# The power of the norms in three parts, and the next image's jobs in other slots

## The chip, the cores and the metric

One core of a Trainium2 chip runs the whole program. The metric is the device time of one execution in microseconds. The kernel before took 2167.36 us (median of three runs, 2160.34 to 2170.95).

## The reference

The program is a small vision tower on 16 images of 3 x 256 x 256, in float32:

```
h = template_match(x)              # 31x31 normalised correlation, mean over 3 channels -> 16 x 256 x 256
t = h * rsqrt(mean(h*h) + eps) * norm_w
q = (t @ Wq)  -> 16 heads of 64;  k, v = (t @ Wkv) -> 8 heads of 64 each
q, k = l2norm(q) * scale_q, l2norm(k) * scale_k       # one norm per token and head
a = softmax(causal(tanh(q k^T / 50) * 50 / 8))        # two query heads share a key head
h = layernorm(h + (a v) @ Wout)
h = layernorm(h + mlp(h))          # three hidden layers of 1024, silu gate, two gelus
```

Each image has 256 tokens of 256 values. For every token the l2norm needs 24 sums of squares (16 query heads, 8 key heads) and their power -1/2.

## The kernel before

There are three stages, one behind the other: the template correlation (`token_stage`), the attention (`attention_stage`) and the three-layer network (`mlp_stage`). The change lies in the attention alone.

Images are taken in four groups of four (`GI` = 4). For an image, the attention has 16 `make` jobs on TensorE: `make 0` to `2` project the first 128 tokens to queries and keys and `make 3` to values, `make 4` to `7` do the same for the other 128 tokens. Each is six matmuls of 512 columns (line 1041). Between them the norms are taken, once per block of 128 tokens, numbered `tb` 0 and 1: ScalarE squares `raw` (line 880); VectorE reduces the squares to 24 sums per token (`sum`, line 933); GpSimd clips them and raises them to -1/2 (`root`, lines 812 and 814); VectorE multiplies queries and keys with them (`scale`, lines 940 and 942, the keys twice). Then `make 8` to `15` transpose the scaled queries and keys (line 1053): 8, 9, 10, 11 need `scale 0`, and 12 to 15 need `scale 1`.

The attention of an image goes head by head, eight of them. For the head numbered n over the group, `score` n is eight matmuls into one of two pairs of `sim` banks (line 1065); ScalarE applies tanh and exp (lines 891 and 894); GpSimd multiplies the diagonal blocks with a triangular mask (line 820); and `mix` (line 1079) multiplies with the values. The mix of head n-2 stands behind the score of head n. All mixes write one PSUM bank, `mixed`. VectorE reads it out with a reciprocal (line 957) and a product (line 959), and the next mix on TensorE waits for that product by `s_mixread`; a sum (line 962) follows.

The engines run one list of steps, `attention_order`, each engine taking from it what is its own, strictly in this order. The list is written out by hand: at head h of an image, behind its score and mix, come the steps of `SLOTS[h]` for the next image. At the first head of an image the mix comes ahead of the score. For the last image of a group the slots lie one head later, and the last slot lies behind the second of the two mixes that follow the last score. The next group's `rms` norm has its sum at the 18th head of a group, its power on GpSimd (lines 804 and 806) two heads later, and its scaling on VectorE (line 921) four heads later. The very first image is made ahead of all heads, by `first_order`. In the list of the final group there is no image to make beside its last image.

Every job writes one of three PSUM banks and waits until the job three before was read out. Queries are read out by ScalarE and keys by VectorE (line 950). DMAs are issued by SyncE alone here, for tokens, results and a scan of words that VectorE folds in with `bits` (line 968).

Of the kernel before, what the change touches and what calls it, by code (L numbers as in the profile page):

```python
# [9 lines left out]
ALU = mybir.AluOpType  # L10
# [21 lines left out]
D, QH, HEADS, DH = SIDE, 16, 8, 64  # L32
# [52 lines left out]
def settle(eng, sem):  # L85

    eng.sem_inc(sem, 1)


def token_stage(nc, sh, X, XT, TF, TPAD, H, WORDS, WEIGHTS, WQKV, NW, GQ, GK):  # L90
# [489 lines left out]


NH = GI * HEADS
SLOTS = (
    [("make", 0), ("make", 1), ("make", 2)],
    [("sum", 0), ("root", 0), ("make", 4)],
    [("make", 5), ("make", 6), ("scale", 0)],
    [("sum", 1), ("root", 1), ("make", 3), ("make", 8)],
    [("make", 9), ("make", 10)],
    [("make", 11), ("make", 7), ("scale", 1)],
    [("make", 12)],  # L590
    [("make", 13), ("make", 14), ("make", 15)],
)


def first_order():

    order = [("turn_h", k) for k in range(4)]
    order += [("make", 0, j) for j in (0, 1, 2)] + [("sum", 0, 0), ("root", 0, 0)]
    order += [("make", 0, j) for j in (4, 5, 6)] + [("scale", 0, 0), ("sum", 0, 1), ("root", 0, 1)]
    order += [("make", 0, j) for j in (3, 7, 8, 9, 10, 11)] + [("scale", 0, 1)]  # L600
    return order + [("make", 0, j) for j in (12, 13, 14, 15)]

# [76 lines left out]
def attention_stage(nc, sh, H, WO, WORDS, X1, fine):  # L679
# [7 lines left out]
    QK = KV + HEADS * DH  # L687
    with ExitStack() as ctx:
# [13 lines left out]
        rn = sb("rn", [P, 2, QK // DH])  # L702
# [19 lines left out]
        s_settle = sh.s_settle  # L722
# [65 lines left out]
        @block.gpsimd  # L788
        def _(pool):
            pool.memset(v[:], 1.0).then_inc(s_const, 1)  # L790
            pool.memset(mask[:], 1.0).then_inc(s_const, 1)
            pool.wait_ge(s_const, 2)
            pool.affine_select(out=mask[:], in_=mask[:], compare_op=ALU.is_ge, fill=0.0, base=0,
                               pattern=[[1, P]], channel_multiplier=-1).then_inc(s_const, 1)
            pool.wait_ge(s_const, 3)

            def emit(run, g):
                for step in run.order:
                    kind = step[0]
                    if kind == "rms_root":  # L800
                        n = g + run.ahead
                        pool.wait_ge(s_hsum, n + 1)
                        settle(pool, s_settle)
                        pool.tensor_scalar(rms[:], ss[:], 1.0 / D, EPS_RMS, ALU.mult, ALU.add).then_inc(s_hmean, 1)
                        pool.wait_ge(s_hmean, n + 1)
                        pool.tensor_tensor(rms[:], rms[:], neg_half[:, 0:PR], ALU.pow).then_inc(s_hroot, 1)
                    elif kind == "root":
                        tb = step[2]
                        t = image(g, step[1]) * 2 + tb
                        pool.wait_ge(s_ss, t + 2)  # L810
                        settle(pool, s_settle)
                        pool.tensor_scalar(rn[:, tb], rn[:, tb], 1e-24, None, ALU.max).then_inc(s_clip, 1)
                        pool.wait_ge(s_clip, t + 1)
                        pool.tensor_tensor(rn[:, tb], rn[:, tb], neg_half[:], ALU.pow).then_inc(s_rn, 1)
                    elif kind == "score":
                        n = step[1]
                        pool.wait_ge(s_exp, g * NH + n + 1)
                        diag = probs[:, n % 4].rearrange("p m (b i) -> p m b i", b=3)[:, :, 0:3:2]
                        both = mask[:].rearrange("p (m b i) -> p m b i", m=1, b=1).to_broadcast([P, 2, 2, P])
                        pool.tensor_tensor(diag, diag, both, ALU.mult).then_inc(s_mask, 1)  # L820
                if run.before:
                    pool.wait_ge(s_aggr, g + 1)
                    settle(pool, s_settle)
                    pool.tensor_scalar(rstd[:], moments[:, :, 1], EPS_LN, None, ALU.add).then_inc(s_lneps, 1)
                    pool.wait_ge(s_lneps, g + 1)
                    pool.tensor_tensor(rstd[:], rstd[:], neg_half[:, 0:PR], ALU.pow).then_inc(s_rstd, 1)

            every_part(pool, emit)
            pool.wait_ge(s_lows, 2)
            pool.partition_all_reduce(lows[:, 1:2], lows[:, 0:1], P, bass.bass_isa.ReduceOp.max).then_inc(s_lows, 1)  # L830
# [76 lines left out]
        def _(dve):  # L907
# [7 lines left out]
            def emit(run, g):  # L915
                for step in run.order:
# [13 lines left out]
                    elif kind == "sum":  # L930
                        tb = step[2]
                        dve.wait_ge(s_sq, image(g, step[1]) * 2 + tb + 1)
                        dve.reduce_sum(rn[:, tb], squares[:, 0:QK].rearrange("p (h d) -> p h d", d=DH), AX_X)\
                           .then_inc(s_ss, 1)
                    elif kind == "scale":
                        tb = step[2]
                        dve.wait_ge(s_rn, image(g, step[1]) * 2 + tb + 1)
                        heads = raw[:, tb].rearrange("p (h d) -> p h d", d=DH)
                        by = rn[:, tb].rearrange("p (h d) -> p h d", d=1)
                        dve.tensor_tensor(heads[:, 0:QH], heads[:, 0:QH], by[:, 0:QH].to_broadcast([P, QH, DH]), ALU.mult)  # L940
                        for m in range(2):
                            ins = dve.tensor_tensor(keys[:, tb, :, m], heads[:, QH:],
                                                    by[:, QH:].to_broadcast([P, HEADS, DH]), ALU.mult)
                        ins.then_inc(s_qn, 1)
                    elif kind == "make" and step[2] >= 8 and step[2] % 4 >= 2:
                        img, tb, r = step[1], step[2] // 4 - 2, step[2] % 4 - 2
                        bank = read_out(run, g, step).rearrange("p (h t) -> p h t", t=P)
                        dve.wait_ge(s_score, image(g, img) * HEADS + 8)
                        by = gamma[:, 4 * r:4 * r + 4].rearrange("p (h t) -> p h t", t=1).to_broadcast([P, 4, P])
                        dve.tensor_tensor(kt[:, img % 2, 4 * r:4 * r + 4, P * tb:P * tb + P], bank, by,  # L950
                                          ALU.mult).then_inc(s_emptied["keys"], 1)
                    elif kind == "mix":
                        n = step[1]
                        img, hd = n // HEADS, n % HEADS
                        got = mixed[:, 0:4 * (DH + 1)].rearrange("p (b m d) -> p b m d", b=2, m=2)
                        dve.wait_ge(s_mix, g * NH + n + 17)
                        dve.reciprocal(rl[:], got[:, :, :, DH:DH + 1]).then_inc(s_rl, 1)
                        dve.wait_ge(s_rl, g * NH + n + 1)
                        dve.tensor_tensor(parts[:], got[:, :, :, 0:DH], rl[:].to_broadcast([P, 2, 2, DH]),
                                          ALU.mult).then_inc(s_mixread, 1)  # L960
                        dve.wait_ge(s_mixread, g * NH + n + 2)
                        dve.tensor_tensor(o[:, img % 2, :, hd], parts[:, :, 0], parts[:, :, 1],
                                          ALU.add).then_inc(s_o, 1)
                    elif kind == "bits":
                        c = g * CHUNKS + step[1]
                        dve.wait_ge(s_words, c * 16 + 16)
                        dve.wait_ge(s_bits, c + 1)
                        dve.tensor_tensor(bits[:], bits[:], words[:], ALU.bitwise_or).then_inc(s_bits, 1)
                    elif kind == "project":
                        k = step[1]  # L970
                        if k == 0:
                            dve.wait_ge(s_h, g * 16 + 16)
                        bank = read_out(run, g, step).rearrange("p (a c) -> p a c", a=2)
                        dve.tensor_tensor(h[:, 2 * k:2 * k + 2], bank, h[:, 2 * k:2 * k + 2], ALU.add)\
                           .then_inc(s_emptied["dve"], 1)
                        dve.wait_ge(s_emptied["dve"], run.emptied_before(g, "dve") + run.counts[run.jobs[step]][1])
                        for a in range(2 * k, 2 * k + 2):
                            ins = dve.bn_stats(stats[:, a], h[:, a])
                        if k == 3:
                            ins.then_inc(s_stats, 1)  # L980
# [542 lines left out]
```

## Time and profile before

| | |
|---|---|
| median of the runs | 2167.36 us |
| profiled execution: time, span | 2172.09, 2170.3 us |
| mean granted TensorE clock over the span | 0.918 |
| TensorE busy | 1915.2 us (88%) |
| VectorE busy | 1214.9 us (56%) |
| ScalarE busy | 854.4 us (39%) |
| GpSimd busy | 773.6 us (36%) |

The page gives for each engine how long it was busy. Of more use here are the views by stage, the waits, and the timelines of each engine. A timeline row has the start in us from the span's start, the duration in us of one instruction or of a run of like ones, engine, line, operation, what was written and read, the count, and in brackets the idle time of the engine just before it, with what ended it. The clock is given as a share of full speed: 1.00 is 2.4 GHz, 0.50 is 1.2 GHz.

### The profile page before, as it was taken

The page shows a single profiled execution, that of the slowest core. Times are in us where ns is not written, and L with a number is a line of the kernel's source. Part 1 is how long each engine was busy: PE and PEld are TensorE (multiplying, and loading weights), DVE is VectorE, ACT ScalarE, POOL GpSimd, SP SyncE. Part 2 cuts the span into 40 slices and gives each one's busy share as a digit, 9 for nine tenths or more (in the row PEclk, how much of TensorE's full clock was granted, in tenths as well). Part 3 has the DMA queues.
Part 4 walks back from the last instruction along what each step waited for, and adds up shares of the span by engine and source line. Part 5 has one row for each costly group of instructions (what it writes and reads, how often), then busy time and mean ns, then how long its engine had stood idle before and what let it go on. Part 6 is the DMA issues. An engine that isn't in the chain of part 4 may idle for free. (4 is left out here: it accounts for less than half of the span.)

```text
span 2170.3 us, 31220 instructions
## 1 busy us (share of the span) xinstructions
PE 1915.2 (88%) x11768; PEld 1651.7 (76%) x11768; DVE 1214.9 (56%) x1671; ACT 854.4 (39%) x1164; POOL 773.6 (36%) x515
## 2 busy tenths in 40 slices
PE   4788998988948988998899899859999999999997
PEld 4788888888946777777778677748787877877876
DVE  7999999899944564565565554532413314134141
ACT  5553443445234563665355545512222212222121
POOL 3223222122254443554254344414333333243332
PEclk9899999999977898897998898879999999999999
DMA  9122212112101000200100010023000000000000
GB/s 143 71 93 77 108 45 91 71 45 117 59 29 53 21 15 8 79 21 14 67 21 21 8 59 14 21 112 144 20 1 19 19 0 19 0 19 20 1 10 11
DMA packets 32211, 95.87 MB, mean 44 GB/s; under 512 B 18630, under 2 KB 18758, under 8 KB 26569
## 3 DMA queue, kind: packets, MB, share of 16 engines
q1 hardware_dynamic: 31500, 89.80, 13.0%
q10 hardware_dynamic: 576, 4.19, 0.5%
q8 instruction: 93, 1.52, 0.3%
q14 instruction: 42, 0.34, 0.0%
HBM read 81.37 MB, written 24.15 MB: 49 GB/s over the span
## 5 line engine op out<-in xcount | busy, mean ns | idle before, releaser
L554 PE MATMUL conv<-w_hi,x_hi 128*128 128x368 f16 (+5 forms) x1320 | 358.0, 280 | 8.5 <-POOL w_lo L262 4.8
L554 PE MATMUL conv<-w_lo,x_hi 128*128 128x368 f16 (+5 forms) x1320 | 358.5, 280 | 0.0
L554 PE MATMUL conv<-w_hi,x_lo 128*128 128x368 f16 (+5 forms) x1320 | 356.8, 280 | 0.0
L820 POOL TENSOR_TENSOR probs<-probs,mask 128x512 f32<-128x512 f32 x128 | 177.6, 1392 | 299.1 <-ACT probs L894 299.1
L1079 PE MATMUL mixed<-v,probs 128*128 128x65 f32 x1536 | 231.2, 308 | 24.2 <-POOL probs L820 15.0
L1079 PEld LDWEIGHTS mixed<-v,probs 128*128 128x128 f32 x1536 | 214.7, 221 | 41.4 <-POOL probs L820 16.8
L1253 POOL TENSOR_TENSOR ha_lo<-raw_c,ha_hi 128x512 fp32r<-128x512 f32 x128 | 165.0, 1289 | 209.9 <-DVE ha_hi L1303 209.9
L1291 ACT ACTIVATE raw_c<-ring,sh 128x512 f32<-128x512 f32 x128 | 88.1, 688 | 372.7 <-PE ring L1388 372.6
L1388 PE MATMUL ring<-ha_hi,wh 128*128 128x512 f32 x512 | 209.4, 409 | 16.8 <-POOL ha_lo L1253 16.8
L554 PEld LDWEIGHTS conv<-w_hi,x_hi 128*128 128x128 f16 x1320 | 192.9, 146 | 17.6 <-issue 9.5
L1388 PE MATMUL ring<-ha_lo,wh 128*128 128x512 f32 x512 | 206.2, 403 | 0.0
L1388 PE MATMUL ring<-hb_hi,wh 128*128 128x512 f32 x512 | 202.5, 396 | 0.0
L1388 PE MATMUL ring<-hb_lo,wh 128*128 128x512 f32 x512 | 201.7, 394 | 0.0
L1303 DVE CAST ha_hi<-raw_c 128x512 fp32r<-128x512 f32 x128 | 80.7, 631 | 213.3 <-ACT raw_c L1291 211.1
L554 PEld LDWEIGHTS conv<-w_hi,x_lo 128*128 128x128 f16 x1320 | 193.4, 147 | 8.4 <-issue 0.3
L554 PEld LDWEIGHTS conv<-w_lo,x_hi 128*128 128x128 f16 x1320 | 193.1, 146 | 8.7 <-issue 0.2
L451 DVE RECIPROCAL rinv<-std 128x2048 f32<-128x2048 f32 x12 | 155.4, 12953 | 0.4
L413 DVE TENSOR_TENSOR_SCAN box<-lines 128x271 f32<-128x271 f32 x192 | 146.1, 834 | 6.7 <-ACT lines L330 6.7
L1303 DVE CAST hb_hi<-raw_c 128x512 fp32r<-128x512 f32 x64 | 27.4, 428 | 216.0 <-ACT raw_c L1291 216.0
L280 POOL TENSOR_TENSOR total<-total,part 128x512 f32<-128x512 f32 x32 | 46.9, 1477 | 262.3 <-DVE part L467 262.3
L891 ACT ACTIVATE probs<-sim 128x768 f32<-128x768 f32 x128 | 103.7, 810 | 93.2 <-PE sim L1065 92.4
L1253 POOL TENSOR_TENSOR hb_lo<-raw_c,hb_hi 128x512 fp32r<-128x512 f32 x64 | 82.5, 1289 | 161.1 <-DVE hb_hi L1303 161.1
(144 smaller groups left out, 3929.2 us busy)
## 6 DMA issues: line engine op xcount, KB each, us to landing
xt<-x_columns_in SPq DMA_DIRECT2D x12, 1163.0 KB, 5.2
xp<-x_patches_in SPq DMA_DIRECT2D x12, 1152.0 KB, 5.1
hidden_words<-hidden_weights_in SPq DMA_DIRECT2D x8, 1408.0 KB, 9.2
words<-hidden_words SPq DMA_DIRECT2D x32, 352.0 KB, 3.1
wh<-hidden_words SPq DMA_DIRECT2D x2, 4096.0 KB, 21.3
tokens<-result ACTq DMA_DIRECT2D x4, 1024.0 KB, 5.3
lines<-tokens SPq DMA_DIRECT2D x4, 1024.0 KB, 5.6
h<-tokens SPq DMA_DIRECT2D x4, 1024.0 KB, 7.7
```

Source lines behind the costliest of these rows:

```text
L280: ins = pool.tensor_tensor(total[:, :, cols], total[:, :, cols], part[:, :, cols], ALU.add)
L413: return dve.tensor_tensor_scan(out, line[:, TH:TH + SCAN], line[:, 0:SCAN], 0.0, ALU.add, ALU.subtract)
L451: dve.reciprocal(rinv[:], std[:]).then_inc(s_point, 1)
L554: ins = pe.matmul(out, xs[:, c, RI - 1 - i:RI - 1 - i + NR, :, x].rearrange("p r g -> p (r g)"), w, start=(t == 0), stop=(t == len(terms) ...
L820: pool.tensor_tensor(diag, diag, both, ALU.mult).then_inc(s_mask, 1)
L891: act.activation(probs[:, n % 4], sim[:, n % 2, :, 0:3 * P], ACT.Tanh, scale=1.0 / CLAMP).then_inc(s_tanh, 1)
L1079: ins = pe.matmul(out, probs[:, n % 4, m, at:at + P], v[:, img % 2, jb, hd], start=(jb == 0), stop=(jb == ib), skip_group_check=True)
L1253: pool.tensor_tensor(dst[1][:, u % KH], raw[:, u % 4], dst[0][:, u % KH].bitcast(F32), ALU.subtract).then_inc(s_lo, 1)
L1291: act.activation(raw[:, u % 4], bank, ACT.Gelu, scale=scale[:, m:m + 1]).then_inc(s_gelu, 1)
L1303: dve.tensor_copy(dst[0][:, u % KH], raw[:, u % 4]).then_inc(s_hi, 1)
L1388: ins = pe.matmul(bank, a, b, start=start, stop=False, skip_group_check=True)
```

## The change

`root` is no longer one step per block of 128 tokens but three (`ROOTS = 3`), each the power of 8 of the 24 columns. The first of the three also does the wait for the sums and the clip. `scale` waits until all three parts of its block are done. The slots are written anew:

```diff
+ROOTS = 3
 SLOTS = (
     [("make", 0), ("make", 1), ("make", 2)],
-    [("sum", 0), ("root", 0), ("make", 4)],
-    [("make", 5), ("make", 6), ("scale", 0)],
-    [("sum", 1), ("root", 1), ("make", 3), ("make", 8)],
-    [("make", 9), ("make", 10)],
-    [("make", 11), ("make", 7), ("scale", 1)],
-    [("make", 12)],
-    [("make", 13), ("make", 14), ("make", 15)],
+    [("sum", 0), ("make", 4), ("root", 0)],
+    [("make", 5), ("make", 6), ("root", 1)],
+    [("root", 2), ("scale", 0), ("sum", 1), ("make", 3)],
+    [("root", 3), ("root", 4), ("make", 7)],
+    [("root", 5), ("make", 8), ("make", 9)],
+    [("scale", 1), ("make", 10), ("make", 11)],
+    [("make", 12), ("make", 13), ("make", 14), ("make", 15)],
 )
```

```diff
 # first_order
-    order += [("make", 0, j) for j in (0, 1, 2)] + [("sum", 0, 0), ("root", 0, 0)]
-    order += [("make", 0, j) for j in (4, 5, 6)] + [("scale", 0, 0), ("sum", 0, 1), ("root", 0, 1)]
+    order += [("make", 0, j) for j in (0, 1, 2)] + [("sum", 0, 0)] + [("root", 0, k) for k in range(ROOTS)]
+    order += [("make", 0, j) for j in (4, 5, 6)] + [("scale", 0, 0), ("sum", 0, 1)] + [("root", 0, ROOTS + k) for k in range(ROOTS)]
```

```diff
 # GpSimd
                     elif kind == "root":
-                        tb = step[2]
+                        tb, part = step[2] // ROOTS, step[2] % ROOTS
                         t = image(g, step[1]) * 2 + tb
-                        pool.wait_ge(s_ss, t + 2)
-                        settle(pool, s_settle)
-                        pool.tensor_scalar(rn[:, tb], rn[:, tb], 1e-24, None, ALU.max).then_inc(s_clip, 1)
-                        pool.wait_ge(s_clip, t + 1)
-                        pool.tensor_tensor(rn[:, tb], rn[:, tb], neg_half[:], ALU.pow).then_inc(s_rn, 1)
+                        size = QK // DH // ROOTS
+                        cols = slice(part * size, part * size + size)
+                        if part == 0:
+                            pool.wait_ge(s_ss, t + 2)
+                            settle(pool, s_settle)
+                            pool.tensor_scalar(rn[:, tb], rn[:, tb], 1e-24, None, ALU.max).then_inc(s_clip, 1)
+                            pool.wait_ge(s_clip, t + 1)
+                        pool.tensor_tensor(rn[:, tb, cols], rn[:, tb, cols], neg_half[:, cols], ALU.pow).then_inc(s_rn, 1)
 # VectorE
-                        dve.wait_ge(s_rn, image(g, step[1]) * 2 + tb + 1)
+                        dve.wait_ge(s_rn, image(g, step[1]) * (2 * ROOTS) + (tb + 1) * ROOTS)
```

The order of the steps on each engine follows from the list: `root 0` to `2` are the parts of the first block, behind the mask products of heads 1, 2 and 3; `root 3` and `4` stand behind that of head 4, and `root 5` behind that of head 5. On VectorE `scale 0` and `sum 1` stand together behind the mix reading of slot 3.

## Rows read from the trace of the kernel before

**Rows 1.** Stages: stretch, its length, busy us of PE, PEld, DVE, ACT, POOL; PEclk; DMA

```profile
670.00:1430.00 760.00, 679.90 (x4137) 578.27 (x4136) 421.67 (x719) 406.20 (x559) 327.68 (x200) 0.87 0.09 28
...
939.65:949.50 9.85, 9.85 (x48) 9.09 (x48) 3.84 (x9) 2.85 (x4) 1.27 (x1) 0.53 0.13 38
```

**Rows 2.** Waits, 670 to 1430: who waited for whom, us in total, times, longest

```profile
PE job L1053 <- DVE keys L942: 39.6, 18, 3.2
...
PE mixed L1079 <- POOL probs L820: 15.0, 8, 3.8
PE mixed L1079 <- DVE parts L959: 9.1, 9, 1.9
```

**Rows 3.** Timeline of TensorE, 921 to 949, the second image of a group

```profile
921.93 0.92 PE L1065 MATMUL sim<-qt,kt 64*128 64x256 f32 x8
...
925.62 0.60 PE L1053 MATMUL job<-ident,raw 128*128 128x128 f32 x4
926.15 0.92 PE L1065 MATMUL sim<-qt,kt 64*128 64x256 f32 x8
...
935.23 1.55 PE L1079 MATMUL mixed<-v,probs 128*128 128x65 f32 x12 [0.76 <-POOL probs L820]
939.65 1.12 PE L1053 MATMUL job<-ident,raw 128*128 128x128 f32 x4 [2.87 <-DVE keys L942]
...
942.28 2.82 PE L1079 MATMUL mixed<-v,probs 128*128 128x65 f32 x12
...
947.45 2.15 PE L1079 MATMUL mixed<-v,probs 128*128 128x65 f32 x12
```

**Rows 4.** Timeline of ScalarE: the exponential of head 3 of the same image

```profile
924.96 0.85 ACT L894 ACTIVATE probs<-probs 128x768 f32<-128x768 f32 x1
```

**Rows 5.** Timeline of GpSimd beside the same image

```profile
917.75 4.19 POOL L814 TENSOR_TENSOR rn<-rn,neg_half 128x24 f32<-128x24 f32 x1
921.91 1.26 POOL L820 TENSOR_TENSOR probs<-probs,mask 128x512 f32<-128x512 f32 x1
...
933.91 5.13 POOL L820 TENSOR_TENSOR probs<-probs,mask 128x512 f32<-128x512 f32 x3
```

**Rows 6.** Timeline of VectorE, 897 to 940

```profile
897.45 1.21 DVE L940 TENSOR_TENSOR raw<-raw,rn 128x1024 f32<-128x1024 f32 x1
...
919.22 0.18 DVE L957 RECIPROCAL rl<-mixed 128x4 f32<-128x4 f32 x1 [2.02 <-PE mixed L1079]
...
919.90 0.29 DVE L962 TENSOR_TENSOR o<-parts 128x128 f32<-128x128 f32 x1
...
921.97 2.29 DVE L940 TENSOR_TENSOR raw<-raw,rn 128x1024 f32<-128x1024 f32 x1 [1.78 <-POOL rn L814]
924.18 1.28 DVE L942 TENSOR_TENSOR keys<-raw,rn 128x512 f32<-128x512 f32 x2
...
927.46 1.74 DVE L933 TENSOR_REDUCE rn<-lines 128x24 f32<-128x1536 f32 x1
...
936.18 3.41 DVE L942 TENSOR_TENSOR keys<-raw,rn 128x512 f32<-128x512 f32 x2
```

**Rows 7.** The group of line 826: durations in ns, least, median, most

```profile
L826 POOL TENSOR_TENSOR rstd<-rstd,neg_half x4: 1662/1665/1668, 867.4 to 1441.8; 128x8 f32<-128x8 f32 x4
```

**Rows 8.** Timeline of TensorE: first, third and fourth images of a group

```profile
877.45 0.92 PE L1065 MATMUL sim<-qt,kt 64*128 64x256 f32 x8
...
904.91 1.45 PE L1079 MATMUL mixed<-v,probs 128*128 128x65 f32 x12
...
964.53 0.92 PE L1065 MATMUL sim<-qt,kt 64*128 64x256 f32 x8
...
992.89 1.64 PE L1079 MATMUL mixed<-v,probs 128*128 128x65 f32 x12
...
1015.96 0.92 PE L1065 MATMUL sim<-qt,kt 64*128 64x256 f32 x8
...
1047.31 1.33 PE L1088 MATMUL job<-ident,o 128*128 128x128 f32 x8
```

## The prediction

> **What bounds the kernel now.** I read the table by stages first, to see where the changed code runs and which engine is full there. The attention stage takes 760 us (670 to 1430); in it TensorE is busy 679.9 us, VectorE 421.7, ScalarE 406.2, GpSimd 327.7, and TensorE's granted clock averages 0.87, so TensorE sets the pace, partly at half rate [rows 1]. The stage of the convolution before it and the three-layer network behind it hold none of the changed steps.
>
> Then the table of waits, for what TensorE waits for. Its longest sums are the transposes of normalised queries behind VectorE's `keys` (39.6 us in 18 waits, the longest 3.2), the mix behind GpSimd's mask product (15.0 in 8, longest 3.8) and the mix behind VectorE's read of the one `mixed` bank (9.1 in 9, longest 1.9) [rows 2]. A wait of `DVE raw` on the power costs nothing by itself; these three do.
>
> Then TensorE's timeline over one image (S3 at 921.93 is the score of head 3; the jobs shown build the next image). Everything follows without a gap until 935.23, where the mix waits 0.76 us for a mask product; `make 12` then waits 2.87 us for the scaled keys, and starts at 939.65 [rows 3]. Behind that the clock falls: from 939.65 to 949.50 it is granted 0.53, that is nearly all at 1.2 of 2.4 GHz [rows 1], a mix takes 2.82 instead of 1.55, a group of four transposes 1.12 instead of 0.60 [rows 3]. So each wait of about 3 us costs its own length and some 4.5 us more. The cause is on GpSimd: a power of 24 columns takes 4.19 us, and the mask products that came ready meanwhile run as a block of three, 5.13 us [rows 5]. They delay the mix, and they slow VectorE: `raw` takes 2.29 beside a mask product and 1.21 without, the two `keys` 3.41 beside the block and 1.28 without [rows 6].
>
> **The change part by part.** *The power in three.* Before, a power of 24 columns is 4.19 us [rows 5], one of 8 columns (that of `rstd`, line 826) 1.67 [rows 7]. Three parts are 5.0 us if each is like that row; 4.2 if only the columns counted. I take 5.0, as it is measured at the very width: +0.8 us for each of 32 powers, 26 us of GpSimd, which is busy 43% of the stage [rows 1]. Beside heads that costs nothing by itself. In the first part, where no head runs, both powers stand in the chain sum, root, scale: +1.6 us (0 to 3).
>
> *The mask products between the parts.* The block of three goes; no mask product waits longer than 3.4 us behind two parts. That removes the 0.76 us wait and up to 3.7 us of the one behind `rms`.
>
> *The spread of the jobs.* `scale 0` moves from head 2 to head 3 and stands directly ahead of `sum 1` there; `make 8` moves from head 3 to head 5, `scale 1` from head 5 to 6, `make 12` from 6 to 7. TensorE's work is the same. The matmuls, copies and DMAs are the same in number; the DMA queue isn't passed by any of it.
>
> What is late next? `scale 0` now waits on the third part, which is queued on GpSimd behind head 3's mask product. VectorE is in order: queued behind `scale 0` are `sum 1` and head 4's mix reading, and the mix of head 5 on TensorE may not write the single `mixed` bank until that reading is done. I replay it on the rows. S3 starts at 921.93 [rows 3]. The exponential of head 3 ends at 925.81, since ScalarE squares the second token block first [rows 4]. Mask product 1.27: 927.1; third part 1.67: 928.8. Now `scale 0`: `raw` 2.29, as head 4's mask product starts at the same moment, `keys` 1.28, `sum 1` 1.74 [rows 6]: 934.1. The mix reading's reciprocal and product are 0.68 (919.22 to 919.90) [rows 6], with the signal 934.9, or S3 + 13.0. TensorE wants it much earlier: a head with one projection job is 926.15 less 921.93 less the 0.53 of `make 8`, 3.7 us; two of them (heads 3 and 4) and the score of head 5, 0.9, give S3 + 8.3 [rows 3]. So TensorE stands still 4.7 us, once per image, where it stood 3.1 to 3.8 us before; without the mask product beside `raw` it is 3.6, with keys also slowed 5.8.
>
> After such a wait the clock is low for about 10 us, as now [rows 1]. From the release: mix 2.6, `make 8, 9` 2.0, score 1.6, mix 2.6, `make 10, 11` 1.6, then at full rate score 0.9, mix 1.4, `make 12` to `15` 2.1 [rows 3]: 15 us (14 to 17). The second normalisation is in time: `sum 1` ends at 934.1, three parts, the clip and one mask product end at 940.9, `scale 1` starts only behind head 6's mix reading, 944.4, and ends at 946.9, where `make 12` is wanted at 947.8. This slack of 0.9 us is thin, and only the low clock makes it.
>
> Start to start, S3 to the next image's first mix, is then 28.0 us. Before it is 25.5 (947.45 less 921.93) [rows 3] in the images like this one, 27.5 in the first image of a group (877.45 to 904.91), 28.4 in the third, where `rms` stands in between (964.53 to 992.89) [rows 8]. Changes: second images and the last group's third, five in all, +2.5 each, 12.5; first images, four, +0.5, 2.0. Third images of the other three groups: the exponential comes 1.4 us later behind the squares of `rms`, but `raw` has no mask product beside it, release at S3 + 13.3, 15 more, and 1.0 for the two `turn_h` at full rate: +1.0 each, 3.0. Fourth images, three, where the slots lie one head later: release at 1028.8, the same path, and a second wait of 2.6 us for the mix reading behind `scale 1` (now there are 0.6, 1.86 and 0.83), to `turn_o` at 1046.7 against 1047.31 [rows 8]: -0.6 each, -1.8. With the 1.6 of the first part the sum is +17 us: 2172.1 to 2189 for an execution like the profiled one. The runs' median is 4.7 us below that execution, and so I put it on 2167.4: **2185 us**.
>
> *A rule weighed.* `raw<-raw,rn` has two SBUF inputs and is held by a mask product that began 0.06 us before it (2.29 against 1.21). `o<-parts` has two as well, and at 919.90 it lies wholly inside the power that runs from 917.75 to 921.94, and takes 0.29 us [rows 5, 6]. I take from this that a power doesn't hold VectorE, and that cutting it frees nothing there. The Trainium skill, "SBUF — State Buffer", in its part on the shared port pair and its single rule, says that whichever of the two engines starts first holds the pair for its whole instruction and the other blocks fully. By the skill's rule `o` would end at 921.94, and thirds would let VectorE in up to 2.5 us sooner; by the row they change nothing. The mask products follow the rule, the power doesn't.
>
> **The rivals.**
> 1. *The wait is paid by the clock* (no change). The idle stretch of 4.7 us takes in more of the low clock than one of 3, so less work meets it. At 8 us of slow work instead of 10 an image has 1 us less, over 15 images 15 us: 2170. For it: the slow stretch is not the same length everywhere. Against: the stretches shown begin where work resumes.
> 2. *The head-5 mix is not held up* (faster, the other side). If head 4's mix reading is done within some 2 us of S3 + 8.3, the clock stays up, as it did at the 0.76 wait [rows 3]; then an image is 18.2 of work (the 25.5 less 3.6 of waits and the 3.7 that the low clock costs ahead of 947.45), 3 of waits at `make 12` and the mix, and 1.5 of slack lost: about 22.7 against 26.8 on average, 15 times: -60, 2107. It decides from a chain at least 2.7 us shorter than mine. For it: the present 7 to 8 us per image lost to wait and clock are real, and the block of masks goes. Against: nothing in the chain from the exponential through mask product, third part, `scale 0` and `sum 1` can start sooner.
> 3. *A second wait at `make 12`* (slower still). It decides once `scale 1` is 0.9 us longer. A mask product beside `raw` adds 1.1, one beside `keys` from 1.1 (half of what the block of three adds there) to 2.1, of which I take 1.6 [rows 6]; less the slack that is 1.8 us an image, 27 us over 15: 2212. For it: GpSimd lags VectorE by a part or two at that point. Against: by my replay the last mask product then ended at 942, before `scale 1` starts.
> 4. *Powers hold VectorE* after all, and thirds free it. One third instead of the whole lies ahead of a two-input instruction, 2.5 us sooner; for half of the 30 powers beside heads that is -37, with my +17: 2147. Against it: 0.29 us inside a power [rows 5, 6]. This is what the Trainium skill's rule in "SBUF — State Buffer" would give.
>
> **How the numbers follow.** Forecast 0.53, rival 1 0.15, rival 2 0.20, rival 3 0.10, rival 4 0.02. The likeliest one's own range is 2174 to 2203: an image off by 1 us is 15 us. Range 2148 to 2213: it takes in rival 1, the centre of rival 3 and the upper edge of rival 2, whose rest is left out, as are the longer sums of rival 3. What this kernel's runs can tell from no change is 0.5%, 10.8 us. Slower: 0.50 of the forecast and rival 3: 0.60. Same: 0.03 of the forecast, 0.13 of rival 1, 0.01 of rival 2: 0.17. The rest, 0.19, 0.02 and rival 4, is faster: 0.23.
>
> **What would show it.** In the profile after: three powers of about 1.67 us for each of 4.19; no block of three mask products; `make 8` with no wait on `keys`; per image one wait of the mix on `DVE parts` of 4 to 5 us, over 60 us in sum where there are 9.1 now [rows 2], and the clock low behind it; each `DVE raw` of the first block beginning behind a third part. Mean clock of the stage near 0.87. I am wrong if the wait on `parts` is under 2 us, if the low stretches become fewer than one an image, or if `make 12` waits 2 us or more again.

## The result

The changed kernel is slower: 2177.5 us (median of 17 runs, 2169.38 to 2198.15) against 2163.84 us (17 runs, 2156.4 to 2170.95) for the kernel before. The ratio is 1.0074, with a 95% interval of 1.0054 to 1.0093, that is about 16 us by the runs' means (the two medians are 13.7 apart), where the prediction added 17 and named 2185.

The profiled execution of the changed kernel took 2178.07 us, close to its own median. That of the kernel before took 2172.09, which is 8 us above the median of its 17 runs. So the two traces differ by 6.1 us in span only (2170.3 to 2176.4), and the account below is of this pair; where the other 10 us come from in the runs without a trace, no trace here can say.

The stage of the attention, first of all. The columns are the stretch, its length, the busy time of PE, PEld, DVE, ACT and POOL, the granted clock, and DMA [rows 1]:

```profile
670.00:1430.00 760.00, 660.17 (x4119) 560.36 (x4118) 391.24 (x716) 409.00 (x561) 341.85 (x260) 0.89 0.09 29
```

TensorE is busy for 20 us less than before in the same 760 us, and its clock is 0.89 instead of 0.87. So it stands still more, and works faster when it works. What it waits for, in the same stretch [rows 2]:

```profile
PE mixed L1083 <- DVE parts L963: 75.6, 27, 4.6
...
DVE raw L944 <- POOL rn L818: 49.5, 15, 4.8
...
PEld mixed L1083 <- POOL probs L824: 14.3, 4, 4.7
PE job L1057 <- DVE keys L946: 8.8, 8, 2.6
```

The matmuls' waits for the keys fell from 39.6 to 8.8 us, and those for a mask product, 15.0 us, left their list. The 14.3 us that the weight loads still have are nearly all three waits of 4.7 at head 5 of the third images, and the matmuls of the same mixes have them, as 4.5, under `DVE parts`; there the two releases lie so close that the profile names one for the load and the other for the matmul. In their place is one wait, for VectorE's reading of `mixed`: 75.6 us, where there were 9.1. The sum of the three went from 63.7 to 84.4, +20.7 us.

One image shows how this comes about: the second of the second group, which [rows 3 to 6] show of before. S3 is at 927.43. TensorE:

```profile
927.43 0.92 PE L1069 MATMUL sim<-qt,kt 64*128 64x256 f32 x8
...
934.99 0.92 PE L1069 MATMUL sim<-qt,kt 64*128 64x256 f32 x8
940.14 2.28 PE L1083 MATMUL mixed<-v,probs 128*128 128x65 f32 x12 [4.22 <-DVE parts L963]
942.21 1.91 PE L1057 MATMUL job<-ident,raw 128*128 128x128 f32 x8
944.05 0.94 PE L1069 MATMUL sim<-qt,kt 64*128 64x256 f32 x8
944.92 1.55 PE L1083 MATMUL mixed<-v,probs 128*128 128x65 f32 x12
...
950.62 1.26 PE L1057 MATMUL job<-ident,raw 128*128 128x128 f32 x8 [0.93 <-DVE keys L946]
...
953.26 1.52 PE L1083 MATMUL mixed<-v,probs 128*128 128x65 f32 x12 [0.35 <-DVE parts L963]
```

ScalarE, the exponential of head 3, and GpSimd [rows 4 and 5]:

```profile
930.46 0.85 ACT L898 ACTIVATE probs<-probs 128x768 f32<-128x768 f32 x1
```

```profile
923.24 1.66 POOL L818 TENSOR_TENSOR rn<-rn,neg_half 128x8 f32<-128x8 f32 x1
925.58 1.29 POOL L824 TENSOR_TENSOR probs<-probs,mask 128x512 f32<-128x512 f32 x1 [0.67 <-ACT probs L898]
926.83 2.29 POOL L818 TENSOR_TENSOR rn<-rn,neg_half 128x8 f32<-128x8 f32 x1
931.38 1.27 POOL L824 TENSOR_TENSOR probs<-probs,mask 128x512 f32<-128x512 f32 x1 [2.26 <-ACT probs L898]
932.61 1.64 POOL L818 TENSOR_TENSOR rn<-rn,neg_half 128x8 f32<-128x8 f32 x1
934.21 1.29 POOL L824 TENSOR_TENSOR probs<-probs,mask 128x512 f32<-128x512 f32 x1
```

And VectorE [rows 6]:

```profile
925.61 2.02 DVE L972 TENSOR_TENSOR bits<-bits,words 128x704 int32<-128x704 int32 x1
...
934.28 2.30 DVE L944 TENSOR_TENSOR raw<-raw,rn 128x1024 f32<-128x1024 f32 x1 [3.44 <-POOL rn L818]
936.50 1.28 DVE L946 TENSOR_TENSOR keys<-raw,rn 128x512 f32<-128x512 f32 x2
937.70 1.74 DVE L937 TENSOR_REDUCE rn<-lines 128x24 f32<-128x1536 f32 x1
939.37 0.17 DVE L961 RECIPROCAL rl<-mixed 128x4 f32<-128x4 f32 x1
939.57 0.42 DVE L963 TENSOR_TENSOR parts<-mixed,rl 128x256 f32<-128x256 f32 x1
```

Read from top to bottom: two thirds are done by 929.1, and GpSimd then idles 2.26 us, since in its order the third one stands behind a mask product whose input isn't there yet. That product runs at 931.38, the third third ends at 934.25, and VectorE, idle for 3.44 us, begins `scale 0` beside the next mask product. `sum 1` and only then the reading of head 4's mix follow; the mix of head 5 begins at 940.14, 12.7 us after S3, having waited 4.22.

The length of what follows: TensorE is back at full rate at 944.05, and not some 9 us after the wait. The window 940.1 to 944.1 is granted 0.58. Behind a wait of the same 4.22 us in the first image of the first group, which ended at 694.66, the slow stretch is 17.5 us long:

```profile
940.10:944.10 4.00, 3.96 (x22) 3.66 (x22) 1.14 (x4) 0.60 (x1) 4.00 (x3) 0.58 0.00 0
694.66:712.20 17.54, 17.54 (x84) 16.08 (x85) 8.54 (x17) 5.70 (x8) 8.64 (x6) 0.51 0.08 21
```

In exchange `make 12` waits 0.93 us here. Over all 15 images it waits 0.93 or 1.00 in six, 0.54 in one, 2.65 in the first image of the second group, and not at all in the other seven. S3 to the next image's first mix is 25.8 us, against 25.5 before.

The first images of the second and third group are another case. `bits`, which folds in words that a DMA brings, stands on VectorE behind head 2's mix reading. Before, `scale 0` stood ahead of it and waited for the power, and `bits` itself never waited (884.30 in the first image of the second group). Now `scale 0` is gone from there, `bits` waits for its words instead, and head 3's mix reading waits behind it, so that TensorE's mix at head 4 stands still 2.75 us, and 1.97 in the third group:

```profile
890.57 0.89 DVE L972 TENSOR_TENSOR bits<-bits,words 128x704 int32<-128x704 int32 x1 [7.61 <-DMA words<-hidden_words]
```

```profile
892.16 2.09 PE L1083 MATMUL mixed<-v,probs 128*128 128x65 f32 x12 [2.75 <-DVE parts L963]
```

The kernels below that have `scale 0` at head 3 or 4 all show this; it was not tested by itself.

### The profile page after: what moved, and what is told of

Same layout as the page of the kernel before. It is cut to its first block and busy times, and to the rows that moved or that the text cites. A ratio compares the mean times of both kernels' runs of the same rounds, so it can differ in the third digit from the quotient of the medians.

```text
span 2176.4 us, 31308 instructions
## 1 busy us (share of the span) xinstructions
PE 1904.6 (88%) x11768; PEld 1643.1 (75%) x11768; DVE 1185.5 (54%) x1671; ACT 855.9 (39%) x1164; POOL 789.0 (36%) x579
## 5 line engine op out<-in xcount | busy, mean ns | idle before, releaser
L1083 PE MATMUL mixed<-v,probs 128*128 128x65 f32 x1536 | 226.5, 304 | 75.7 <-DVE parts L963 75.6
L1083 PEld LDWEIGHTS mixed<-v,probs 128*128 128x128 f32 x1536 | 209.4, 216 | 92.7 <-issue 68.7
L824 POOL TENSOR_TENSOR probs<-probs,mask 128x512 f32<-128x512 f32 x128 | 167.1, 1305 | 275.2 <-ACT probs L898 275.2
L818 POOL TENSOR_TENSOR rn<-rn,neg_half 128x8 f32<-128x8 f32 x96 | 162.7, 1701 | 2.7
L961 DVE RECIPROCAL rl<-mixed 128x4 f32<-128x4 f32 x128 | 22.8, 178 | 224.6 <-PE mixed L1083 224.6
```

The lines of the kernel that those rows point to most:

```text
L818: pool.tensor_tensor(rn[:, tb, cols], rn[:, tb, cols], neg_half[:, cols], ALU.pow).then_inc(s_rn, 1)
L1083: ins = pe.matmul(out, probs[:, n % 4, m, at:at + P], v[:, img % 2, jb, hd], start=(jb == 0), stop=(jb == ib), skip_group_check=True)
```

## The experiments

All ratios are against the kernel before, run on the same chip among them. Three theories stood: **A**, the loss is the mix reading that stands behind `scale 0` and `sum 1` while a third is awaited; **B**, it is the fixed cost of three powers instead of one; **C**, it is the later `make` jobs.

**e1, thirds in place.** The old slots, three thirds back to back.

```diff
-    [("sum", 0), ("root", 0), ("make", 4)],
+    [("sum", 0), ("root", 0), ("root", 1), ("root", 2), ("make", 4)],
-    [("sum", 1), ("root", 1), ("make", 3), ("make", 8)],
+    [("sum", 1), ("root", 3), ("root", 4), ("root", 5), ("make", 3), ("make", 8)],
```

> The slots of before with the three thirds back to back where the whole power stood. Theory A (the loss comes from where scale 0 and sum 1 stand, behind a third that is queued behind head 3's mask product, so that head 4's mix reading and with it TensorE's mix wait): the changed kernel's waits on DVE parts are absent, 10 us or less in sum; only the 0.8 us per power is added, in the chain sum, power, scale, so two scales 0.8 us later in each of 15 images and 1.6 us ahead of them: about +24 us on before, ratio 1.011 (1.004 to 1.016). Theory B (the thirds' fixed cost is the whole loss): the same time as the changed kernel, ratio 1.0074, as nothing but the thirds is in both. Theory C (the later makes are the loss): 1.000 to 1.003.

Measured: 2182.25 us, ratio 1.0102 (1.0062 to 1.0142). The waits, 670 to 1380:

```profile
PE job L1057 <- DVE keys L946: 40.8, 21, 3.9
...
PE mixed L1083 <- POOL probs L824: 18.8, 6, 5.2
...
PE mixed L1083 <- DVE parts L963: 9.5, 10, 1.9
```

The waits on `parts` are near those of before (9.5 us, where before has 7.4 in the same stretch), and the kernel is as slow as A's 1.011 says: three powers in a row lengthen the chain of sum, power and scale. The wait for the keys in the first images is 3.8 us instead of 3.1, that of the mix on the mask product in the third images 5.16 instead of 3.75. This interval overlaps that of the changed kernel, so the time alone doesn't refute B, but the waits are quite others than the changed kernel's: it loses by its thirds in another place. The cost of thirds is real where they stand in a chain.

**e2, the new slots with the whole power.**

```diff
-ROOTS = 3
+ROOTS = 1
-    [("make", 5), ("make", 6), ("root", 1)],
-    [("root", 2), ("scale", 0), ("sum", 1), ("make", 3)],
-    [("root", 3), ("root", 4), ("make", 7)],
-    [("root", 5), ("make", 8), ("make", 9)],
+    [("make", 5), ("make", 6)],
+    [("scale", 0), ("sum", 1), ("make", 3)],
+    [("root", 1), ("make", 7)],
+    [("make", 8), ("make", 9)],
```

> The new slots with the power whole (ROOTS = 1): root 0 behind head 1's mask product, root 1 behind head 4's. Theory A: the power of the first block is done some 3 us ahead of head 3's mix reading, so scale 0 starts right behind that reading, sum 1 ends about 8.1 us after S3 and head 5's mix waits 0.4 us instead of 4.2; make 12 waits about 1 us. The clock stays up. S3 to the next image's first mix 20 to 21 us where the changed kernel has 26 to 28: 5 to 6.5 us less in 15 images, ratio to before 0.96 to 0.97, 2080 to 2100 us. Theory B: the time of before, 1.000, with the thirds gone. Theory C (the spread itself costs): as slow as the changed kernel or slower, 1.007 or more.

Measured: 2129.88 us, ratio 0.9841 (0.9808 to 0.9873). The waits, 670 to 1380:

```profile
PE mixed L1083 <- DVE parts L963: 30.0, 21, 3.6
PE job L1057 <- DVE keys L946: 27.4, 12, 2.9
```

C falls: the same spread of jobs, without the thirds, gains 34 us. B's 1.000 is missed as clearly. A's direction holds and its size was too large: head 5's mix waits 0.70 in second images, where 0.4 was reckoned, up to 1.0 in first ones and 2.2 in fourth ones, and `make 12` waits 2.2 to 2.9 in eleven of the 15 images instead of about 1. The longest waits of first images, 3.19 and 2.09, are at head 4, behind `bits`.

**e3, `sum 1` ahead of `scale 0`.** The changed kernel with two steps in the other order.

```diff
-    [("root", 2), ("scale", 0), ("sum", 1), ("make", 3)],
+    [("root", 2), ("sum", 1), ("scale", 0), ("make", 3)],
```

> The changed kernel with sum 1 ahead of scale 0 in slot 3 on VectorE: the 1.74 us of the sum run while scale 0's third is still awaited. Theory A: head 5's mix waits 4.2 less 1.7, 2.5 us, and the second block's thirds start 1.7 us or more sooner. If the clock stays high after 2.5 us, an image has 5 us less (ratio to before 0.975), if it falls as before, 1.7 us less, 25 us in all: 2152, ratio 0.995. Theory B and C: no difference to the changed kernel, 1.0074.

Measured: 2145.09 us, ratio 0.9908 (0.9877 to 0.9939), between A's two cases and clear of B's and C's. Nothing is taken away, and 1.74 us of VectorE that stood in the wait now run ahead of it: head 5's mix waits 2.6 us in second images, where 2.5 was expected, and the waits on `parts` are 52.9 us up to 1380, where the changed kernel has 69.4.

**e4, `scale 0` behind head 4's mix reading.** The thirds stay.

```diff
-    [("root", 2), ("scale", 0), ("sum", 1), ("make", 3)],
-    [("root", 3), ("root", 4), ("make", 7)],
+    [("root", 2), ("sum", 1), ("make", 3)],
+    [("scale", 0), ("root", 3), ("root", 4), ("make", 7)],
```

> The changed kernel with sum 1 alone in slot 3 and scale 0 moved behind head 4's mix reading, thirds kept. Theory A: head 5's mix doesn't wait for the reading any more (waits on DVE parts under 15 us in sum); make 8 waits about 1 us for the keys and make 12 about 1 us; 5 to 6 us less than the changed kernel in each of 15 images, ratio to before 0.96 to 0.97. Theory B: 1.0074, as the same thirds are there. Theory C: 1.0074 or more.

Measured: 2130.68 us, ratio 0.9852 (0.9822 to 0.9883). With all its thirds the kernel gains 33 us on before, so B isn't the cause. The waits, 670 to 1380:

```profile
PE job L1057 <- DVE keys L946: 43.5, 25, 4.6
...
PE mixed L1083 <- DVE parts L963: 21.0, 10, 4.3
```

The waits on `parts` fell to 21.0, not under 15. Head 5's mix isn't in them any more: 13.0 are a second wait of 4.3 in each fourth image, and 5.2 the two at head 4 behind `bits`. `keys` took 43.5: `make 8` waits 0.65 to 0.78 us, as expected, but `make 12` waits 2.7 in first and second images and 4.6 in third ones instead of about 1, since `scale 1` hangs on a third that is queued behind head 5's mask product. The gain was half of what was expected, and these waits are the likely reason.

**e7, one third moved.** The changed kernel with `root 2` behind `root 1`, ahead of head 3's mask product.

```diff
-    [("make", 5), ("make", 6), ("root", 1)],
-    [("root", 2), ("scale", 0), ("sum", 1), ("make", 3)],
+    [("make", 5), ("make", 6), ("root", 1), ("root", 2)],
+    [("scale", 0), ("sum", 1), ("make", 3)],
```

> The changed kernel with one third moved: root 2 from slot 3, behind head 3's mask product, to slot 2, behind root 1. All thirds, all makes, both scales and sums as in the changed kernel. Theory A: scale 0 starts right behind head 3's mix reading, 3.4 us sooner, the wait of head 5's mix falls from 4.2 to about 1 us, and the time to about that of e2: ratio 0.980 to 0.990. If instead the length of scale 0 and sum 1 on VectorE were enough to hold the mix, the wait stays 3 us or more: 1.000 to 1.007.

Measured: 2149.8 us, ratio 0.993 (0.9905 to 0.9955). This is the most direct test, as 8 of 24 columns change place by one instruction and nothing else. The wait of head 5's mix in the second group's second image, and the one at `make 12` behind it:

```profile
924.11 1.52 PE L1083 MATMUL mixed<-v,probs 128*128 128x65 f32 x12 [0.70 <-DVE parts L963]
...
934.69 1.39 PE L1057 MATMUL job<-ident,raw 128*128 128x128 f32 x8 [2.63 <-DVE keys L946]
```

The wait fell from 4.22 to 0.70 us, and the kernel is faster than before the change. The ratio lies between my two ranges, for two reasons. The time won at head 5 is in part lost at `make 12`, 2.63 where it was 0.93: the second scale was late all along and hid behind the first wait. And the wait falls to 0.70 only in second images and the last group's third, five of 15. In the first images of the first and last group it is 2.70, in third images 3.16 and in fourth ones 2.83, instead of 4.2 and 4.5. In a third image the two thirds still stand behind a mask product that comes late, that of head 2:

```profile
956.01 1.27 POOL L824 TENSOR_TENSOR probs<-probs,mask 128x512 f32<-128x512 f32 x1 [3.80 <-ACT probs L898]
957.24 3.24 POOL L818 TENSOR_TENSOR rn<-rn,neg_half 128x8 f32<-128x8 f32 x2
```

The waits on `parts` up to 1380 are 40.8 us, where the changed kernel has 69.4.

**e5, e6: what the spread is worth without that wait.** e5 is e2 with `sum 1` first and the second power ahead of head 4's mask product; e6 moves `scale 0` as well.

```diff
 # e5, against e2
-    [("scale", 0), ("sum", 1), ("make", 3)],
-    [("root", 1), ("make", 7)],
+    [("sum", 1), ("root", 1), ("scale", 0), ("make", 3)],
+    [("make", 7)],
 # e6, against e5
-    [("sum", 1), ("root", 1), ("scale", 0), ("make", 3)],
-    [("make", 7)],
+    [("sum", 1), ("root", 1), ("make", 3)],
+    [("scale", 0), ("make", 7)],
```

> e2's whole powers, with sum 1 ahead of scale 0 and root 1 moved from slot 4 into slot 3, ahead of head 4's mask product. e2 measured 0.984, with make 12 waiting 2.2 to 2.9 us in each image and the low clock behind it. If that wait comes from root 1 being queued behind head 4's mask product and sum 1 behind scale 0, the second power starts about 2.5 us sooner, the mask products are through before scale 1, and the waits of make 12 fall under 1 us; the wait at head 5 stays at 0.7 us: 2 to 4 us less an image, ratio 0.960 to 0.975. Rival: the mask products of heads 4 and 5, now behind the power, hold the mixes of heads 6 and 7 instead (over 15 us of mix on POOL probs): 0.98 to 0.99.

Measured for e5: 2096.93 us, ratio 0.9700 (0.9671 to 0.9729). The waits for keys are 4.0 us up to 1340, so the two edits together take away `make 12`'s wait of e2; what each of them is worth wasn't told apart. The rival was partly right too: mixes wait 17.0 us on mask products.

> e5 with scale 0 moved behind head 4's mix reading. By theory A nothing of the normalisation is then ahead of a mix reading that TensorE is about to need: the waits on DVE parts under 15 us in sum, make 8 and make 12 under 1 us each, clock 0.94 or more over the span: ratio 0.950 to 0.970. Rival: scale 0 ends too late for make 8, which then waits as it did before the change, 1 to 3 us: 0.975 to 0.985.

Measured for e6: 2089.19 us, ratio 0.9660 (0.9632 to 0.9688). This beats both kernels: 3.4% faster than before, with the same arithmetic on every engine, in another order. Its stage, and one image of it, TensorE at full rate throughout:

```profile
670.00:1340.00 670.00, 617.88 (x4112) 521.62 (x4111) 383.20 (x716) 403.69 (x558) 313.71 (x200) 0.95 0.10 32
896.00:918.00 22.00, 20.64 (x161) 17.50 (x162) 15.32 (x29) 13.72 (x18) 12.46 (x9) 1.00 0.12 34
```

`make 8` and `make 12` wait about 1 us at most, as expected. The waits on `parts` are 19.5 us, where under 15 was expected: 3.44 behind `scale 1` in each fourth image, about 2 at head 4 of two first images, behind `bits`, and small ones. The mix waits 2.83 on a mask product in the three third images that have the `rms` power ahead of it.

**e8, `rms` one head later.** e6 with `RMS_AT + 2` and `+ 4` made `+ 3` and `+ 5`.

> e6 (0.966) with the power of the rms norm one head later (RMS_AT + 3) and its scaling too (RMS_AT + 5). In e6 the third images keep a wait of 2.8 us of the mix on the mask product of head 4, which lies behind root 1 and the rms power. If that is their cause, this wait goes in 3 images, with some of the low clock behind it: 5 to 15 us less, ratio 0.960 to 0.964. Rival: the 5 us of rms scaling on VectorE then lie ahead of a later mix reading that TensorE needs: 0.966 or more.

Measured: 2096.42 us, ratio 0.9682 (0.9656 to 0.9709). There is no gain, as by the rival, but not for its reason. The matmuls' waits on mask products fell from 8.5 to 2.5 us as forecast, those on `parts` are about the same (20.8 after 19.5), and those on keys rose from 10.3 to 17.8: `make 12` now waits 3.08 us in the three third images. There `scale 1` runs beside mask products that came out late from behind the `rms` power, 2.29 and 2.35 us long where e6's undisturbed `scale 0` takes 1.22 and 1.29.

**e9, thirds well placed.** e6's places with the power in thirds.

```diff
-ROOTS = 1
+ROOTS = 3
-    [("make", 5), ("make", 6)],
-    [("sum", 1), ("root", 1), ("make", 3)],
-    [("scale", 0), ("make", 7)],
+    [("make", 5), ("make", 6), ("root", 1), ("root", 2)],
+    [("sum", 1), ("root", 3), ("make", 3)],
+    [("scale", 0), ("root", 4), ("root", 5), ("make", 7)],
```

> e6 with the power again in thirds, placed so that none is awaited behind a mask product that comes late: root 0 behind head 1's mask, roots 1 and 2 behind head 2's, root 3 behind head 3's, roots 4 and 5 behind head 4's. If a division of the power is worth something in itself (mask products of heads 4 and 5 sooner, and the rms power with them), it is under e6: 0.960 to 0.964. Theory A, by which placing decides and TensorE needs none of those mask products sooner: 0.964 to 0.970, and the fixed cost of the thirds shows only ahead of the heads (+2 us). If the thirds' cost of 0.8 us a power reached TensorE in every image, 0.972 or more.

Measured: 2099.61 us, ratio 0.9698 (0.9672 to 0.9724). It is at the far end of A's range; the intervals of e6 and e9 overlap, and their medians, taken on two chips, are 10 us apart. No gain from dividing the power is seen where its place is right.

The table has them side by side. The last columns but one are the matmuls' waits on `parts`, keys and mask products together, and the granted clock, both from 670 to 1340 us.

| kernel | power | `root 2` or power 0 ahead of head 3's mask | `scale 0` at head | waits, us | clock | ratio |
|---|---|---|---|---|---|---|
| before | whole | yes | 2 | 58.3 | 0.88 | 1 |
| changed | thirds | no | 3 | 78.2 | 0.91 | 1.0074 |
| e1 | thirds | yes | 2 | 68.6 | 0.88 | 1.0102 |
| e2 | whole | yes | 3 | 56.8 | 0.93 | 0.9841 |
| e3 | thirds | no, `sum 1` first | 3 | 56.6 | 0.91 | 0.9908 |
| e4 | thirds | no, `sum 1` first | 4 | 65.5 | 0.93 | 0.9852 |
| e7 | thirds | yes | 3 | 60.0 | 0.90 | 0.9930 |
| e5 | whole | yes, `sum 1` first | 3 | 40.6 | 0.95 | 0.9700 |
| e6 | whole | yes, `sum 1` first | 4 | 38.3 | 0.95 | 0.9660 |
| e8 | whole | as e6, `rms` later | 4 | 41.1 | 0.95 | 0.9682 |
| e9 | thirds | yes, `sum 1` first | 4 | 46.3 | 0.96 | 0.9698 |

The sum of the waits doesn't order the kernels by itself. e4 waits longer than the kernel before and is 1.5% faster: many of its waits are short, and its clock is 0.93 instead of 0.88.

## Why the prediction was right

*The thirds.* Forecast 1.67 us each from the row of `rstd` [rows 7]; the trace has, in ns:

```profile
L818 POOL TENSOR_TENSOR rn<-rn,neg_half x96: 1628/1662/2296, 646.0 to 1387.4; 128x8 f32<-128x8 f32 x96
```

In the first part the forecast was +1.6 us; the second head's score starts 2.0 us later (674.4 against 672.4).

*What goes.* The block of three mask products is gone, and with it the matmuls' wait on them. `make 8` doesn't wait beside heads. Both as forecast.

*What is late next.* The replay gave a release of head 5's mix at S3 + 13.0 and a wait of 4.7 us; it is 12.7 and 4.22, and in the third images 4.54. `raw` beside the mask product was put at 2.29 and is 2.30, and `sum 1` at 1.74 is 1.74. The waits on `parts`, forecast as over 60 us in sum, are 75.6. 13 of the 15 images have a wait of 4.1 to 4.6 at head 5. That this wait is what makes the change a loss is shown by e7, e3 and e4, which each take it away or shorten it in another manner, keep all the thirds, and are all faster than before.

*The sizes that were off.* The low clock behind the wait was put at over 8.8 us of slow work in every image; in the image above it is 3.9, in the first group's first image 17.5. And `make 12` was put without a wait, thanks to that slow stretch; it waits in eight images, 0.93 us in the one above. The two partly cancel there: 25.8 us from S3 to the next mix where 28.0 was forecast. The second wait of the fourth images, put at 2.6, is 3.35 to 3.44. By kind of image, from score to score of the second heads and added up, in the traced pair: first images +4.0 us in four (forecast +2.0); second images and the last third, -0.4 in five (forecast +12.5); other third images +1.2 in three (forecast +3.0); fourth images +0.3 in three (forecast -1.8). With the first part's 2.0 that is +7 at the last projections (1423.05 to 1430.03), where the forecast was +17. So the sum for the traced pair was ten too high, mostly in the term of second images.

What that term lacks lies behind the point where the forecast stops counting. From S3 to the next image's first mix these five images are 9.6 us longer together, near the 12.5 of the forecast. From that mix to the second head's score they are 10.0 us shorter. The kernel before is late in the image with its wait, at `make 12`, and its low clock lasts into the next image; the changed kernel has its wait 5 us earlier in the image and is at full rate again by then. This is the stretch in the first group's second image, before and then after, 9.2 and 7.0 us for the same work:

```profile
748.62:757.84 9.22, 9.22 (x39) 7.50 (x39) 1.67 (x5) 2.85 (x4) 1.30 (x1) 0.69 0.00 0
```

```profile
756.39:763.40 7.01, 6.63 (x40) 5.32 (x38) 2.40 (x6) 2.74 (x4) 1.53 (x2) 1.00 0.19 51
```

The forecast had put the low clock behind its own wait into the sum, and took the one behind the old wait as ending with the image. First images were counted from one as well: the 27.5 us of before is the second group's, the other three took 25.1 to 26.1, and so from S3 to the mix the four are 5.7 us longer together and not 2.0.

The change by all runs, +16, is close to the forecast because the traced execution of before was 8 us above the median of its runs, and that of the changed kernel at its own. How long the clock stays low isn't the same from image to image, and I had one trace of it. So part of the nearness of 2185 to 2177.5 is luck, while the sign isn't.

*What it had no term for.* The prediction had the DMAs out of it ("the DMA queue isn't passed by any of it"). It didn't look at what else had stood behind the wait of `scale 0` at head 2: `bits` waits 7.61, 6.83 and 3.14 us for its words in the first images of the last three groups, and in two of them TensorE waits behind it, 4.7 us together.

*The rivals.* Rival 1, that the clock pays for the wait, is partly seen: the stage's clock rose to 0.89 and less work met the low rate, the 10.0 us above included; but it didn't pay for all of it. Rival 2 needed head 4's reading within 2 us of S3 + 8.3. I had said that nothing in that chain could start sooner, which is right for the changed kernel. Where an edit lets it (e7, e2), the wait does fall to 0.70 in second images; but the gain is 0.7 and 1.6%, not 2.8, since other images keep a wait and `make 12` then waits. Rival 3 is seen small, about 0.93 us in most images that have it; in one it is 2.65, over the 2 us that I had named as a sign of being wrong. Rival 4 isn't borne out (below); in weighing it I wrote that `o` would end at 921.94 by the rule, where it would begin there.

## What to carry to other kernels

A step that is cut in parts and threaded between other work ends when its last part does, and the last part inherits the wait of whatever is queued ahead of it: here 8 of 24 columns waited for an exponential, and the kernel took 1.0074 of the time of before, where the same spread with the power in one piece (e2) took 0.9841. Follow, on the consumer's engine, what stands behind the consumer: the loss was not in the scale but in a 0.6 us bank reading queued behind it. A longest wait hides the next one, so after each shift read the waits again, and for every kind of image, since an edit that frees one kind can leave another waiting. Count the low clock to its end: here it ran on past the image in which the wait stood. Moves in a list of steps, without one instruction less, were worth 3.4%.

## What the runs showed of the hardware

GpSimd's power keeps VectorE out only while it begins. In e6 `raw` and both `keys`, with two SBUF inputs each, lie beside a power of 24 columns and take their undisturbed 1.22 and 1.29 us:

```profile
901.67 4.19 POOL L818 TENSOR_TENSOR rn<-rn,neg_half 128x24 f32<-128x24 f32 x1
```

```profile
903.16 1.22 DVE L944 TENSOR_TENSOR raw<-raw,rn 128x1024 f32<-128x1024 f32 x1
904.29 1.29 DVE L946 TENSOR_TENSOR keys<-raw,rn 128x512 f32<-128x512 f32 x2
```

In all 11 traces `o` (two SBUF inputs, 0.29 us) lies wholly inside a power some 300 times and is never longer. Where an instruction starts with the power, the delay is small: `o` takes 0.35 us when it starts 0.03 us after the power does (929.78 in the trace of before), and `raw` 1.26 when it starts 0.17 after it (939.72 in e6).

The other way round there is contention: in the changed kernel the second third, 2.29 instead of 1.66, was issued at 926.83 while VectorE's `bits` ran to 927.63, itself 2.02 us instead of 0.88 behind a mask product. The rows fit a hold that lasts while GpSimd reads its inputs, all of a mask product's 512 columns but only 24 of the power's; that reading is argued from these rows and wasn't tested by itself. The Trainium skill, "SBUF — State Buffer", section "SBUF: two separate sides", has the pair held for the whole instruction. The mask products agree with it (`raw` 2.30 us beside one), the power doesn't.

The clock: waits of 0.92 and 0.35 us didn't lower it (e6, granted 1.00 over 896 to 918). Those of 4.2 lowered it, and the slow stretch behind them was 3.9 us at 940.14, 6.0 at 1293.02 and 17.5 at 694.66, in one execution of the changed kernel.
